# Moving the first normalisation's aggregation to GpSimd, pairing two small operations, and a new instruction order in a one-core attention and feed-forward kernel

## The chip, the cores and the metric

The kernel runs on one core of one Trainium2 chip. The metric is the device time of one execution in microseconds (us): 80.45 us is the median of three runs before the change (80.34 to 80.68). The five engines are called as in the profile: PE (TensorE, matrix products), DVE (VectorE), ACT (ScalarE), POOL (GpSimd) and SP (SyncE, which here only issues DMAs). Each runs its own list of instructions strictly in the order written, and they meet only through semaphores.

## What is computed

x is 4 x 256 x 256, the context 4 x 256 x 128. `fp8` is rounding to float8 e4m3, simulated in float32.

```python
def layernorm(x, eps=1e-5): return (x - mean(x)) / sqrt(var(x) + eps)

def attention(xn, ctx, Wq, bq, Wk, bk):
    q, k = ctx @ Wq.T + bq, ctx @ Wk.T + bk        # 256 x 128 for each of 4 batches
    a = softmax(q @ k.T)
    return xn @ a.T                                 # 256 x 256

def quantised_linear(qx, sx, sc, W, idx):           # rows of W scaled to 448 and rounded to fp8
    ws = max(abs(W[:, idx]), axis=1) / 448
    return qx * sx @ (fp8(W[:, idx] / ws) * ws).T * sc

def ffn(x):                                         # hidden size 704
    qx, sx, sc = quantise(x, up_index)              # per row: peak, scale to 448, round to fp8
    t = silu(quantised_linear(qx, ..., w_gate)) * quantised_linear(qx, ..., w_up)
    return quantised_linear(*quantise(t, down_index), w_down)

x = x + attention(layernorm(x), ctx, ...)
x = x + ffn(layernorm(x))
```

## The kernel before

The 1024 rows of x are 8 tiles of 128 rows (T = 8, two per batch: LT = 2); HB = 2 batches make a half, so most small row statistics are handled for four tiles at once. The hidden size of 704 makes KC = 6 chunks of 128 of the gate and up weights.

There are two stages. **The front** (about the first 37 us) does attention for four batches and, woven between, quantises the weights. For each batch b: `scores(b)` on PE, `score_max(b)` on DVE, `exps(b)` on ACT, `reciprocal_of_z(b)` and `spread_of_z(b)` on DVE (the identity times 1/z, one 128 x 128 block for each half of the rows), `transpose_att(b)` on PE (a product with that block, which transposes and divides at once), `evac_attT(b)` on ACT, `attend(b)` on PE, and `residual(b)` on DVE, which multiplies by the first normalisation's `rstd1` and adds x. `rstd1` needs `bn_stats1` and `bn_aggr1` on DVE and `add_eps1` and `rstd1_of` on POOL. Then the second normalisation (`bn_stats2`, `bn_aggr2`, `centre_x1`), the row peaks and the rounding of x (`grids_x`, `add_grid_x` on DVE, `subtract_x(b)` on POOL), `transpose_qx(b)` on PE and `evac_qxT(b)` on ACT. Each weight chunk k goes `peak_of_up` and `scales_up` (DVE), `scale_up` (ACT), `exponents_up` and `floor_up` (DVE, in pairs of chunks), `add_grid_up` and `subtract_up(k)` (POOL, 128 x 512), `dequantise` (ACT), `transpose_up` (PE), `evac_up` (ACT) and `split_up` (DVE). The down weights are peaked by `peak_of_down`, rounded, transposed by DMA, permuted by POOL's six indirect DMAs (`scatter`) and read back from DRAM (lines 331 to 333).

**The loop over tiles** (from about 37.5 us) starts with `gates(0)`, which waits for `evac_qxT(0)` and for the last `split_up(5)`. For each tile i: `gates(i)` and `ups(i)` on PE (16 products of 352 columns), `silu(i)` on ACT, `hidden(i)`, `peak_of_t`, `reciprocal_t`, `scales_t`, `grids_t`, `add_grid_t` on DVE, `subtract_t(i)` on POOL, `transpose_t(i)` on PE, `evac_tT(i)` on ACT, `down(i)` on PE, `scale_y(i)` on DVE (with `yscale_of(i)` from POOL: row factor times peak), and `add_residual(i)` on POOL or DVE. `keep_clock`, `keep_warm` and `keep_busy` are products on zeros whose results nobody reads.

The order on every engine is written out by hand as a list of calls at the end of each engine's function (POOL from line 438, ACT from 619, DVE from 954, PE from 1283, SP's loads from 308). An instruction waits at the head of its queue until its semaphores are up, and all behind it wait as well.

## Time and profile before

| | |
|---|---|
| median of 3 runs | 80.45 us (80.34 to 80.68) |
| the profiled execution's own time | 80.45 us |
| its span, first to last instruction | 78.6 us |
| outside the span | 1.85 us |
| busy: PE, DVE, ACT, POOL | 69.5, 69.1, 52.0, 54.1 us |
| instructions of DVE and of POOL | 180 and 66 |
| granted clock | 1.00 |

A duration in the profile is from the start of an instruction to the end of its writes, and instructions of one engine overlap a little, so the room that an instruction takes on its engine is read from its start to the next one's start. That distance is called its slot in this document. Matrix products are pipelined, so a busy PE need not be PE at its peak.

### The profile page before, as it was taken

Reading aid. Unit: us, or ns where it says so; the run is one execution under the profiler, and the core shown is the slowest. Engines: PE = TensorE matmul, PEld = TensorE weight load, DVE = VectorE, ACT = ScalarE, POOL = GpSimd, SP = SyncE. Lnnn points to the kernel's source line nnn. Section 1 sums busy time; section 2 is a strip of 40 time slices with the busy share of each in tenths; the row PEclk is TensorE's granted clock in tenths of the full one; section 3 lists DMA queues with packets and bytes.
Section 4 is the critical chain, followed back from the end, with each engine's and each line's share of the span. In section 5 each row is a group of like instructions: output and inputs, shape, how many; then the busy total and the mean of one; then the engine's idle time right before and its main releaser. Section 6 shows DMA issues by size and latency. Waiting matters only on the chain.

```text
span 78.6 us, 1481 instructions
## 1 busy us (share of the span) xinstructions
PE 69.5 (88%) x449; PEld 57.7 (73%) x449; DVE 69.1 (88%) x180; ACT 52.0 (66%) x102; POOL 54.1 (69%) x66
## 2 busy tenths in 40 slices
PE   4999998999749599294999999999799999985996
PEld 4945837988549489272998999979698699744575
DVE  1019999999899999999999999999999999999860
ACT  0615799999966999897877472937924557446400
POOL 5000008973999999985687989899954667985960
DMA  0899999900000000004140201110033001030143
GB/s 18 289 389 388 330 360 397 379 20 0 0 4 4 0 0 8 0 0 91 32 77 0 75 0 33 33 38 0 17 88 112 4 22 53 0 133 0 41 159 133
DMA packets 6839, 7.33 MB, mean 93 GB/s; under 512 B 2256, under 2 KB 5200, under 8 KB 6832
## 3 DMA queue, kind: packets, MB, share of 16 engines
q1 hardware_dynamic: 6064, 5.97, 23.1%
q10 hardware_dynamic: 576, 0.92, 3.3%
q0 software_dynamic: 192, 0.36, 1.5%
q8 instruction: 3, 0.05, 0.3%
q14 instruction: 4, 0.03, 0.1%
HBM read 5.44 MB, written 1.41 MB: 87 GB/s over the span
## 4 chain that ended last, share of the span: by engine, by line
DVE 30%; POOL 25%; PE 22%; issue 15%; DMA 6%; SPq 1%; POOLq 0%; DVEq 0%
POOL q_w L407 6%; DVE t_sb L885 6%; DMA x_sb<-x_dram 6%; PE gate_ps L1197 5%; PE up_ps L1197 5%; DVE peak_w L820 4%; POOL rstd L371 3%; PE gate_ps L1269 3%; POOL sum_w L403 3%; POOL x_sb L435 3%; POOL yscale L417 2%; DVE grid_w L772 2%; PE bank_c L1154 2%; POOL q_t L424 2%; DVE peak_d L850 2%
## 5 line engine op out<-in xcount | busy, mean ns | idle before, releaser
L403 POOL TENSOR_TENSOR sum_w<-sum_w,grid_w 128x512 f32<-128x512 f32 x5 | 5.7, 1155 | 11.9 <-DVE grid_w L777 11.9
L424 POOL TENSOR_TENSOR q_t<-sum_t,grid_t 128x704 bf16<-128x704 f32 x7 | 10.9, 1554 | 3.9 <-DVE sum_t L915 3.9
L1197 PE MATMUL gate_ps<-w_hi,qxT 128*128 128x352 f32 x32 | 10.7, 337 | 1.2 <-issue 1.2
L1197 PE MATMUL up_ps<-w_hi,qxT 128*128 128x352 f32 x32 | 10.8, 340 | 0.4 <-DVE t_sb L885 0.4
L590 ACT ACTIVATE act_g<-gate_ps,rowscale 128x704 f32<-128x704 f32 x8 | 6.7, 843 | 5.3 <-PE gate_ps L1197 5.3
L1197 PE MATMUL gate_ps<-w_lo,qxT 128*128 128x352 f32 x32 | 10.3, 323 | 0.0
L1197 PE MATMUL up_ps<-w_lo,qxT 128*128 128x352 f32 x32 | 10.3, 323 | 0.0
L604 ACT ACTIVATE tT<-bank_b 128x768 bf16<-128x768 bf16 x7 | 5.7, 809 | 5.6 <-PE bank_c L1241 3.2
L1154 PE MATMUL bank_c<-attT,xT 128*128 128x256 f32 x32 | 7.7, 383 | 1.5 <-DVE x L758 1.5
L357 POOL DMA_INDIRECT wdnT_order<-wdnT,idx_sb x6 | 7.0, 1164 | 1.6 <-issue 1.6
L597 ACT ACTIVATE abs_t<-t_sb 128x704 bf16<-128x704 f32 x8 | 6.3, 786 | 2.4 <-DVE t_sb L885 2.4
L1154 PEld LDWEIGHTS bank_c<-attT,xT 128*128 128x128 f32 x32 | 5.8, 190 | 2.4 <-issue 1.7
L1197 PEld LDWEIGHTS gate_ps<-w_hi,qxT 128*128 128x128 f32 x32 | 6.0, 188 | 1.7 <-issue 1.4
L885 DVE TENSOR_TENSOR t_sb<-up_ps,act_g 128x704 f32<-128x704 f32 x8 | 7.1, 887 | 0.1
L915 DVE SCALAR_TENSOR_TENSOR sum_t<-t_sb,s_t,grid_t 128x704 f32<-128x704 f32 x7 | 6.9, 984 | 0.3
L890 DVE TENSOR_REDUCE peak_t<-t_sb 128x1 f32<-128x704 f32 x8 | 7.0, 881 | 0.0
L713 DVE BATCH_NORM_STATS2 bn<-x_sb 128x6 f32<-128x256 f32 x8 | 3.0, 413 | 4.5 <-DMA x_sb<-x_dram 4.5
L407 POOL TENSOR_TENSOR q_w<-sum_w,grid_w 128x512 bf16<-128x512 f32 x6 | 6.8, 1161 | 0.2
L1197 PEld LDWEIGHTS up_ps<-w_hi,qxT 128*128 128x128 f32 x32 | 6.0, 188 | 0.8 <-ACT qxT L547 0.7
L1197 PEld LDWEIGHTS up_ps<-w_lo,qxT 128*128 128x128 f32 x32 | 6.0, 188 | 0.0
L1197 PEld LDWEIGHTS gate_ps<-w_lo,qxT 128*128 128x128 f32 x32 | 6.0, 188 | 0.0
L566 ACT ACTIVATE sum_w<-q_w,peak_w 128x256 f32<-128x256 bf16 x12 | 5.2, 507 | 1.1 <-POOL q_w L407 1.1
(105 smaller groups left out, 190.8 us busy)
## 6 DMA issues: line engine op xcount, KB each, us to landing
x_sb<-x_dram SPq DMA_DIRECT2D x4, 256.0 KB, 8.7
xT<-x_t_dram SPq DMA_DIRECT2D x2, 512.0 KB, 8.9
out_dram<-x_sb SPq DMA_DIRECT2D x8, 128.0 KB, 1.7
wup_sb<-w_gate_up_dram ACTq DMA_DIRECT2D x3, 256.0 KB, 5.7
wup_sb<-w_gate_up_dram SPq DMA_DIRECT2D x3, 256.0 KB, 5.9
wdn_sb<-w_down_dram SPq DMA_DIRECT2D x1, 704.0 KB, 9.3
ctx_sb<-ctx_t_dram SPq DMA_DIRECT2D x2, 256.0 KB, 4.8
wdnT_in_order<-wdnT_order SPq DMA_DIRECT2D x1, 320.0 KB, 2.8
```

Of the source, the lines that this page charges most:

```text
L357: nc.gpsimd.indirect_dma_start(out=wdnT_order, out_offset=bass.IndirectOffsetOnAxis(ap=idx_sb[0:fresh[k], k:k + 1], axis=0), in_=wdnT[0:fr ...
L403: nc.gpsimd.tensor_tensor(sum_w[:, k], sum_w[:, k], grid_w[:, k], ALU.add).then_inc(sum_w_done[k], 1)
L407: nc.gpsimd.tensor_tensor(q_w[:, k], sum_w[:, k], grid_w[:, k], ALU.subtract).then_inc(q_w_done, 1)
L424: nc.gpsimd.tensor_tensor(q_t[:, i % 2], sum_t[:, i % 2], grid_t[:, i % 2], ALU.subtract)\
L590: nc.scalar.activation(halves(act_g[:, i % 3]), gate_ps[:, :, 0:IH], ACT.Silu, scale=rowscale[:, i:i + 1]).then_inc(silu_done, 1)
L597: nc.scalar.activation(abs_t[:, i % 2], t_sb[:, i % 2], ACT.Abs, scale=GRID)\
L604: nc.scalar.activation(tT[:, i % 2], tT_ps, ACT.Copy).then_inc(tT_evac, 1)
L885: nc.vector.tensor_tensor(halves(t_sb[:, i % 2]), up_ps[:, :, 0:IH], halves(act_g[:, i % 3]), ALU.mult).then_inc(t_done, 1)
L890: nc.vector.tensor_reduce(peak_t[:, i:i + 1], t_sb[:, i % 2], AX_X, ALU.max, apply_absolute_value=True).then_inc(peak_t_done, 1)
L915: nc.vector.scalar_tensor_tensor(sum_t[:, j], t_sb[:, j], s_t[:, col], grid_t[:, j], ALU.mult, ALU.add)\
L1154: last = nc.tensor.matmul(xm_ps[:, j], xT[:, b, c, j * P:(j + 1) * P], attT[:, b, c], start=(c == 0), stop=(c == NC - 1))
L1197: last = nc.tensor.matmul(ps[:, h, 0:IH], qxT[:, b, c, j * P:(j + 1) * P].bitcast(F32R), w[:, c, a, h * IH:(h + 1) * IH].bitcast(F32R), st ...
```

## The change

It has four parts. (1) `bn_aggr1` is gone from DVE (8 instructions). POOL makes the variance itself from the raw statistics of four tiles at once, with five small instructions in place of one (`sum_of_halves`, `halves_apart`, `square_apart`, `weigh_apart`, `add_eps1`); it gives N times the variance, and the factor is put back where `attT` is copied out (`evac_attT` now scales by sqrt(N), with the mean's constant to match). (2) `spread_of_z` is one 128 x 256 product with broadcast operands in place of two of 128 x 128. (3) `yscale_of` handles tiles 0 to 5 in pairs, so there are 5 instructions in place of 8. (4) The order of the calls changes on all engines, and three of SP's loads swap places.

```diff
+        apart1 = sb("apart1", [P, T])
+        both1 = sb("both1", [P, T])
+        square1 = sb("square1", [P, T])
...
             load_up(5)
+            load_down()
             load_x(1)
-            load_down()
+            load_x(3)
             load_x(2)
-            load_x(3)
             load_xT(1)
...
-            def add_eps1(h):
+            def halves_apart(h):
                 four = slice(HB * LT * h, HB * LT * (h + 1))
                 pool.wait_ge(stats1_done, HB * (h + 1))
-                step(nc.gpsimd.tensor_scalar(ve1[:, four], mv1[:, four, 1], LN_EPS, 1.0, ALU.add, ALU.mult),
-                     ("ve1", h))
+                step(nc.gpsimd.tensor_tensor(apart1[:, four], bn1[:, four, 1], bn1[:, four, 4], ALU.subtract),
+                     ("apart1", h))
+
+            def sum_of_halves(h):
+                four = slice(HB * LT * h, HB * LT * (h + 1))
+                pool.wait_ge(stats1_done, HB * (h + 1))
+                step(nc.gpsimd.tensor_tensor(both1[:, four], bn1[:, four, 2], bn1[:, four, 5], ALU.add), ("both1", h))
+
+            def square_apart(h):
+                four = slice(HB * LT * h, HB * LT * (h + 1))
+                after(("apart1", h))
+                step(nc.gpsimd.tensor_tensor(square1[:, four], apart1[:, four], apart1[:, four], ALU.mult),
+                     ("square1", h))
+
+            def weigh_apart(h):
+                four = slice(HB * LT * h, HB * LT * (h + 1))
+                after(("square1", h))
+                step(nc.gpsimd.tensor_scalar(square1[:, four], square1[:, four], N / 4.0, N * LN_EPS, ALU.mult, ALU.add),
+                     ("weighed1", h))
+
+            def add_eps1(h):
+                four = slice(HB * LT * h, HB * LT * (h + 1))
+                after(("weighed1", h))
+                after(("both1", h))
+                step(nc.gpsimd.tensor_tensor(ve1[:, four], both1[:, four], square1[:, four], ALU.add), ("ve1", h))
...
-            def yscale_of(i):
+            def yscale_of(first, last):
...
             add_grid_up(0)
             add_grid_up(1)
             subtract_up(0)
             subtract_up(1)
+            sum_of_halves(0)
+            halves_apart(0)
+            square_apart(0)
+            weigh_apart(0)
             add_eps1(0)
-            add_grid_up(5)
             rstd1_of(0)
             add_grid_up(2)
             subtract_up(2)
+            halves_apart(1)
             add_grid_up(3)
+            square_apart(1)
+            weigh_apart(1)
+            add_grid_up(5)
             subtract_up(3)
             subtract_up(4)
             subtract_up(5)
+            sum_of_halves(1)
             add_eps1(1)
             rstd1_of(1)
             add_eps2(0)
             rstd2_of(0)
+            subtract_x(0)
             rowscale_of(0)
-            subtract_x(0)
...
+            subtract_t(1)
             subtract_x(3)
-            subtract_t(1)
-            yscale_of(0)
-            yscale_of(1)
+            yscale_of(0, 1)
+            yscale_of(2, 3)
             scatter(5)
             subtract_t(2)
             subtract_t(3)
+            yscale_of(4, 5)
             subtract_t(4)
             add_residual(0)
-            yscale_of(2)
+            add_residual(1)
+            yscale_of(6, 6)
             subtract_t(5)
-            yscale_of(3)
-            yscale_of(4)
-            yscale_of(5)
-            yscale_of(6)
-            add_residual(1)
             subtract_t(6)
+            yscale_of(7, 7)
             subtract_last(0)
-            yscale_of(7)
...
-                nc.scalar.activation(attT[:, b], attT_ps, ACT.Identity, bias=minus_mean[:, 0:1])\
+                nc.scalar.activation(attT[:, b], attT_ps, ACT.Identity, bias=minus_mean[:, 0:1],
+                                     scale=float(N) ** 0.5)\
...
-                for j in range(2):
-                    last = nc.vector.tensor_scalar(spread_rz[:, b, j], ident_ps, rz[:, b, j:j + 1], None, ALU.mult)
-                last.then_inc(spread_rz_done[b], 1)
+                nc.vector.tensor_tensor(spread_rz[:, b], ident_ps.unsqueeze(1).to_broadcast([P, 2, P]),
+                                        rz[:, b].unsqueeze(2).to_broadcast([P, 2, P]), ALU.mult)\
+                    .then_inc(spread_rz_done[b], 1)
...
             bn_stats1(0)
-            bn_aggr1(0)
             peak_of_up(0)
             peak_of_up(1)
+            peak_of_up(2)
             reciprocal_up(0)
-            peak_of_up(2)
             scales_up(0)
             peak_of_up(3)
+            reciprocal_up(1)
             peak_of_up(4)
+            scales_up(1)
             score_max(0)
-            reciprocal_up(1)
             exponents_up(0)
+            floor_up(0)
+            peak_of_up(5)
+            reciprocal_of_z(0)
+            spread_of_z(0)
             score_max(1)
...
```

The rest of DVE's new order up to the loop over tiles, as it stands after the change, one call after the other: reciprocal_up(2), peak_of_down, reciprocal_of_z(1), scales_up(2), spread_of_z(1), bn_stats1(1), reciprocal_down, bn_stats1(2), exponents_up(1), scales_down, exponents_up(2), floor_up(1), floor_up(2), bn_stats1(3), residual(0), score_max(2), bn_stats2(0), split_up(0), score_max(3), add_grid_up(4), reciprocal_of_z(2), bn_aggr2(0), spread_of_z(2), residual(1), split_up(1), reciprocal_of_z(3), peak_of_x(0), bn_stats2(1), spread_of_z(3), reciprocal_x(0), bn_aggr2(1), split_up(2), grids_down(0), scales_x(0), grids_down(1), grids_x(0), add_grid_down(0), add_grid_x(0), split_up(3), residual(2), add_grid_down(1), bn_stats2(2), split_up(4), peak_of_x(1), bn_aggr2(2), reciprocal_x(1), residual(3), split_up(5). In the loop, scale_y(1) now stands ahead of scales_t(5), and peak_of_x(3) ahead of hidden(0).

On PE, `place_ident` moves from ahead of `project_k(0)` to behind `scores(0)`. `attend(3)` moves ahead of `transpose_qx(0)`, three `keep_clock(2)` stand ahead of `gates(0)` and those between `gates(2)` and `transpose_t(0)` are gone (their number in all is unchanged), `down(2)` and `transpose_t(4)` move ahead of the `keep_busy` calls, and two `keep_busy` move from the end to ahead of `transpose_t(6)`. On ACT, `dequantise(1)`, `dequantise(2)` and `evac_up(0)` move ahead of `exps(2)` and `exps(3)` (`absolute_down(0)` behind them), and `silu(i)` moves ahead of `absolute_t(i - 1)` for tiles 2 and 4.

## Rows read from the trace of the kernel before

**Rows 1.** The page, its part on busy time of each engine.

```profile
PE 69.5 (88%) x449; PEld 57.7 (73%) x449; DVE 69.1 (88%) x180; ACT 52.0 (66%) x102; POOL 54.1 (69%) x66
```

**Rows 2.** Busy time of each engine by stretches of the span.

```profile
core 0: us, PE busy (x) PEld busy (x) DVE busy (x) ACT busy (x) POOL busy (x), PEclk, DMA share, GB/s
...
20.00:33.00 13.00, 9.18 (x61) 8.07 (x60) 12.64 (x42) 11.65 (x30) 12.43 (x14) 1.00 0.01 3
33.00:37.50 4.50, 3.16 (x20) 2.43 (x20) 4.50 (x14) 3.41 (x7) 3.28 (x3) 1.00 0.23 43
37.50:74.00 36.50, 34.84 (x256) 30.32 (x256) 35.66 (x83) 22.39 (x33) 29.25 (x35) 1.00 0.14 38
```

**Rows 3.** The chain of waits: start us, us, what.

```profile
9.77 0.60 DVE neg_max L737
...
37.53 1.52 PE gate_ps L1197 x8
```

**Rows 4.** DVE's instructions in order of time: start us, busy us, what.

```profile
13.80 0.30 DVE L718 BATCH_NORM_AGGREGATE mv<-bn 128x2 f32<-128x6 f32 x2
14.02 0.14 DVE L764 RECIPROCAL rec_w<-peak_w 128x4 f32<-128x4 f32 x1
...
21.66 0.88 DVE L758 SCALAR_TENSOR_TENSOR x<-bank_c,rstd,x_sb 128x256 f32<-128x256 f32 x2 [0.35 <-POOL rstd L371]
...
25.27 0.86 DVE L758 SCALAR_TENSOR_TENSOR x<-bank_c,rstd,x_sb 128x256 f32<-128x256 f32 x2
...
27.30 0.23 DVE L718 BATCH_NORM_AGGREGATE mv<-bn 128x2 f32<-128x6 f32 x2
27.45 0.58 DVE L749 TENSOR_SCALAR spread_rz<-up_ps,rz 128x128 f32<-128x128 f32 x2
27.94 0.68 DVE L785 TENSOR_REDUCE peak_x<-xT 128x2 f32<-128x512 f32 x1
...
30.12 0.94 DVE L868 SCALAR_TENSOR_TENSOR sum_d<-wdn_sb,s_d,grid_d 128x704 f32<-128x704 f32 x1
...
37.02 0.42 DVE L875 TENSOR_TENSOR w_lo<-bank_a,w_hi 128x256 fp32r<-128x256 f32 x1
37.35 0.24 DVE L718 BATCH_NORM_AGGREGATE mv<-bn 128x2 f32<-128x6 f32 x2
...
75.56 0.48 DVE L946 SCALAR_TENSOR_TENSOR y_sb<-bank_a,yscale,down_scale 128x256 f32<-128x256 f32 x1 [0.47 <-PE bank_a L1259]
```

**Rows 5.** POOL's instructions in order of time: start us, busy us, what.

```profile
12.14 2.27 POOL L403 TENSOR_TENSOR sum_w<-sum_w,grid_w 128x512 f32<-128x512 f32 x2 [10.25 <-DVE grid_w L777]
...
16.75 0.58 POOL L365 TENSOR_SCALAR ve<-mv 128x4 f32<-128x4 f32 x1
18.94 1.16 POOL L403 TENSOR_TENSOR sum_w<-sum_w,grid_w 128x512 f32<-128x512 f32 x1 [1.62 <-DVE grid_w L777]
20.05 1.50 POOL L371 TENSOR_TENSOR rstd<-ve,minus_half 128x4 f32<-128x4 f32 x1
...
28.59 0.19 POOL L365 TENSOR_SCALAR ve<-mv 128x4 f32<-128x4 f32 x1
...
30.13 0.99 POOL L378 TENSOR_SCALAR ve<-mv 128x4 f32<-128x4 f32 x1
...
32.31 0.20 POOL L390 TENSOR_TENSOR rowscale<-rstd,peak_x 128x2 f32<-128x2 f32 x1
32.47 1.16 POOL L396 TENSOR_TENSOR q_x<-sum_x,grid_x 128x512 bf16<-128x512 f32 x1
```

**Rows 6.** Groups of instructions by shape: busy us, mean ns of one.

```profile
L417 POOL TENSOR_TENSOR yscale<-rowscale,peak_t 128x1 f32<-128x1 f32 x8 | 2.7, 361 | 0.0
```

**Rows 7.** The loads' and the down weights' issues on SP's queue.

```profile
4.54 0.47 SPq L303 DMA_DIRECT2D wdn_sb<-w_down_dram  x1
...
57.24 0.39 SPq L331 DMA_DIRECT2D wdnT_in_order<-wdnT_order  x1
```

**Rows 8.** PE, the first product of the down weights.

```profile
60.83 0.93 PE L1241 MATMUL bank_c<-wdnT_in_order,tT 128*128 128x256 bf16 x6
```

More of the change, by code:

```diff
@@ L411, in subtract_down @@
                 nc.gpsimd.tensor_tensor(q_d[:, j, 0:I], sum_d[:, j], grid_d[:, j], ALU.subtract).then_inc(q_d_done, 1)
-            def yscale_of(i):
-                pool.wait_ge(peak_t_done, i + 1)
-                pool.wait_ge(rowscale_done, i // LT + 1)
-                nc.gpsimd.tensor_tensor(yscale[:, i:i + 1], rowscale[:, i:i + 1], peak_t[:, i:i + 1], ALU.mult)\
+            def yscale_of(first, last):
+                tiles = slice(first, last + 1)
+                pool.wait_ge(peak_t_done, last + 1)
+                pool.wait_ge(rowscale_done, last // LT + 1)
+                nc.gpsimd.tensor_tensor(yscale[:, tiles], rowscale[:, tiles], peak_t[:, tiles], ALU.mult)\
                     .then_inc(yscale_done, 1)
@@ L661, in _ @@
             evac_qxT(0)
+            evac_up(5)
             absolute_x(1)
-            evac_up(5)
             centre_x1(2)
+            centre_x1(3)
+            silu(0)
             absolute_x(2)
-            silu(0)
-            centre_x1(3)
             silu(1)
@@ L722, in bn_stats1 @@
                 dve.wait_ge(x_in[b], 16)
-                bn_stats(1, x_sb, bn1, b)
-            def bn_aggr1(b):
-                bn_aggr(1, bn1, mv1, stats1_done, b)
+                for j in range(LT):
+                    last = nc.vector.bn_stats(bn1[:, LT * b + j], x_sb[:, b, j])
+                last.then_inc(stats1_done, 1)
             def bn_stats2(b):
@@ L980, in _ @@
             spread_of_z(1)
-            peak_of_down()
+            bn_stats1(1)
             reciprocal_down()
+            bn_stats1(2)
             exponents_up(1)
             scales_down()
+            exponents_up(2)
             floor_up(1)
-            exponents_up(2)
             floor_up(2)
+            bn_stats1(3)
+            residual(0)
             score_max(2)
+            bn_stats2(0)
+            split_up(0)
             score_max(3)
             add_grid_up(4)
-            bn_stats1(2)
-            residual(0)
-            bn_aggr1(2)
-            bn_stats2(0)
-            split_up(0)
             reciprocal_of_z(2)
-            reciprocal_of_z(3)
             bn_aggr2(0)
             spread_of_z(2)
-            bn_stats1(3)
             residual(1)
             split_up(1)
+            reciprocal_of_z(3)
+            peak_of_x(0)
             bn_stats2(1)
-            bn_aggr1(3)
             spread_of_z(3)
-            peak_of_x(0)
+            reciprocal_x(0)
             bn_aggr2(1)
-            reciprocal_x(0)
+            split_up(2)
             grids_down(0)
             scales_x(0)
-            split_up(2)
+            grids_down(1)
             grids_x(0)
             add_grid_down(0)
-            grids_down(1)
             add_grid_x(0)
@@ L1017, in _ @@
             residual(2)
-            peak_of_x(1)
+            add_grid_down(1)
             bn_stats2(2)
             split_up(4)
-            add_grid_down(1)
+            peak_of_x(1)
+            bn_aggr2(2)
             reciprocal_x(1)
@@ L1024, in _ @@
             split_up(5)
-            bn_aggr2(2)
             bn_stats2(3)
@@ L1284, in _ @@
             keep_warm(WARM_UP)
-            place_ident()
             project_k(0)
@@ L1289, in _ @@
             scores(0)
+            place_ident()
             scores(1)
@@ L1293, in _ @@
             keep_clock(2)
-            keep_clock(2)
             transpose_att(0)
@@ L1297, in _ @@
             keep_clock(2)
+            spread()
             transpose_att(1)
-            spread()
+            attend(0)
             scores(2)
+            transpose_up(0)
             scores(3)
-            attend(0)
-            transpose_up(0)
             attend(1)
             transpose_up(1)
+            keep_clock(2)
+            keep_clock(2)
             transpose_att(2)
             transpose_up(2)
-            attend(2)
             keep_clock(2)
             keep_clock(2)
+            attend(2)
             transpose_up(3)
@@ L1313, in _ @@
             transpose_up(4)
+            attend(3)
             transpose_qx(0)
-            attend(3)
             transpose_up(5)
+            keep_clock(2)
+            keep_clock(2)
+            keep_clock(2)
             gates(0)
@@ L1345, in _ @@
             ups(7)
+            down(2)
+            transpose_t(4)
             keep_busy(0)
             keep_busy(1)
-            transpose_t(4)
-            down(2)
             keep_busy(2)
+            transpose_t(5)
             down(3)
             down(4)
-            transpose_t(5)
+            keep_busy(3)
+            keep_busy(4)
             transpose_t(6)
```

83 lines of the change are left out of this document (35 added, 48 removed).

## Prediction

> **What bounds the kernel now.** I began with the page's busy times [rows 1]: PE and DVE stand level at 69 us of a 78.6 us span, POOL at 54. Such shares mix stages, so the busy times by stretch came next [rows 2]. From 20 to 33 us DVE is busy 12.64 of 13.00 us and POOL 12.43; from 33 to 37.5 DVE is busy all 4.50 us, while PE has only 3.16; in the loop over tiles DVE has 35.66 of 36.50 us and PE 34.84. The reader should see that DVE never rests, that POOL runs beside it at the same pressure in the second half of the front, and that PE joins them in the loop. The chain of waits [rows 3] says the same: it runs through DVE's queue at the start (one piece, a score_max of 0.60 us, is shown) and goes through `gates(0)` at 37.53. Last I read DVE's own queue in order of time [rows 4]. `gates(0)` starts right behind DVE's `split_up(5)` (37.02 to 37.44), and the only DVE wait near the end is 0.47 us before the last `scale_y`, at 75.56, behind the tail of transposes and products. So a slot taken out of DVE ahead of 37 us should bring the end forward by as much, unless POOL or PE takes over.
>
> **What the change takes from DVE.** *Aggregation.* Eight instructions go, in four pairs. A pair's slot is 14.02 - 13.80 = 0.22 us or 27.45 - 27.30 = 0.15 us [rows 4]; I count two of each, 0.74 us. *Diagonals.* A pair of 128x128 products has a slot of 27.94 - 27.45 = 0.49 us, four pairs 1.96 us. The 128x256 product that replaces a pair, one operand in PSUM and both broadcast, is not in the trace. The nearest row is L875's 128x256 form, also a tensor_tensor with one operand in PSUM: 37.35 - 37.02 = 0.33 us of slot. The upper bound is L758, a 256-column product from PSUM with a third operand, two in 0.86 us, or 0.43 each. I take 0.33, since the operation and the memory agree: 4 x (0.49 - 0.33) = 0.64 us saved, at the upper bound 0.24. A gain beyond 0.33 has no row for it; the small DVE instructions alone take 0.15 us and 256 columns cannot be cheaper than 128 (half a pair, 0.25), which gives at most 0.96. DVE loses 1.38 us in all (0.98 to 1.70). Dropping the semaphore steps between the `bn_stats1` pairs I cost at nothing, either way: they ran back to back.
>
> **What it adds to POOL.** POOL gets ten small instructions in place of two [rows 5]. Their prices in the trace spread widely: `ve` (128x4) took 0.58, 0.19 and 0.99 us, `rowscale` 0.20, the eight `yscale` 0.36 on average [rows 6]. I take 0.36 and 0.08 for the waits between them, 0.44 each; the bounds are 0.20 and 0.99. The first five fall where POOL idled anyway, 1.62 us ahead of the `add_grid_up` at 18.94 [rows 5], and POOL now starts earlier: of what DVE did ahead of `floor_up(0)`, a pair of `bn_aggr1` (0.22) and `score_max(1)` (0.60) [rows 3] are gone or later and a `scales_up` (0.07) is added, so POOL's first `add_grid_up` comes at about 12.14 - 0.75 = 11.4. Four products of 1.14 bring it to 15.95, which is also about when DVE has done `bn_stats1(1)`. Five small ones take it to 18.1 and the power of 0.9 to 1.5 us [rows 5] to 19.0 to 19.6, where it was 21.55. DVE reaches `residual(0)` at about 19.3; behind it all of DVE's queue would wait, at most 0.3 us, and before it waited 0.35 at the same place [rows 4]. (Where DVE stands in the new order I get by adding up the slots of its new list.)
>
> From 19.3 POOL has, up to the end of `subtract_x(0)`: three `add_grid_up` and four `subtract_up` of about 1.15 (8.05), five small (2.2), the power `rstd1(1)` (1.25), `ve2` (1.0 as at 30.13), `rstd2` (1.1) and `subtract_x(0)` (1.15), together 14.75, so 34.05. Before it was 32.47 + 1.16 = 33.63. `rowscale(0)` (0.20) is moved behind it, which is in the sum. So the small instructions use up the lead that POOL won. What waits for it: `transpose_qx(0)` on PE, now behind `attend(3)`, and behind that `transpose_up(5)`, then ACT's `evac_qxT(0)` and `evac_up(5)`, then `split_up(5)`: by the rows of their kind 0.4 + 0.6 + 0.5 + 0.4 + 0.4, so 2.3 us to 36.35. DVE's own queue would be through `split_up(5)` at 37.44 - 1.38 = 36.06, and it carries one `bn_aggr2` (0.15) earlier than before: 36.2. POOL is thus late by about 0.15 to 0.4 us, and that is what I take back from the saving.
>
> **Edits at nothing.** *Loads.* `load_down` is issued ahead of `load_x(1)`, and `load_x(3)` ahead of `load_x(2)`. They are issued from 4.54 us on [rows 7]. The w_down data comes earlier by one x load, and so does its reader: `peak_of_down` now stands ahead of `bn_stats1(1)`. The x load that is now last is read by `bn_stats1(2)`, near 16 us. If DVE met data still in flight, it would lose some tenths; I count none. *`yscale` in pairs.* Three fewer small POOL instructions, and none of them between `subtract_t(5)` and `subtract_t(6)`. This opens room on POOL in a stage where DVE sets the pace, so no gain. *Down weights.* They are read back from 57.24 [rows 7] and first used at 60.83 [rows 8]. The `scatter` chain hangs on POOL; it keeps its length and starts with `subtract_down(1)`, which no longer waits as long for DVE. To come 1.0 us forward in the loop, `down(0)` needs this chain about 0.5 us earlier, an estimate; POOL gets there by about 0.8. *`keep_clock` and `place_ident`.* The same number of filler products, three sets now ahead of `gates(0)`; PE has 1.3 us free there [rows 2]. *`scale_y(1)`* moves forward ahead of `scales_t(5)`; it takes a slot of 0.4 that DVE pays either way, and `down(1)` is just done then.
>
> **The sum.** 1.38 saved on DVE, less 0.35 for `split_up(5)` held by POOL's late `subtract_x(0)` and small new waits in the loop: 1.03 us. The profiled execution took 80.45 us, 1.85 of it outside its span, and the median is the same 80.45. Forecast **79.4 us**, a span of 77.6.
>
> **Rivals.**
> *A, forecast (0.52):* DVE's saved slots come through but for some tenths; 78.9 to 79.9.
> *B, the gain is not passed on (0.20):* another queue holds the loop where it was. For it: PE is at 34.84 of 36.50 us there, close behind DVE [rows 2], and the down weights come only just ahead of `down(0)`. If the read-back does not move, the loop can gain no more than about 0.5 us; with the upper bound for the diagonals (0.4 less) nothing measurable is left. 80.0 to 80.7, middle 80.3. Against it: PE's filler products leave it slack.
> *C, slower by POOL's small instructions (0.14):* five of them stand between `rstd1(0)` and `rstd1(1)`, where POOL is full. At 0.99 each (30.13, while DVE ran the two-input product of 30.12 to 31.06 [rows 4, 5]) instead of 0.44 they add 2.75 us, `split_up(5)` ends at 39.1 in place of 37.44, and the time is 80.45 + 1.7 = 82.1. The point at which it decides: `subtract_x(0)` must end later than 35.1, that is the five must cost 0.66 each with their waits; the mean of the twelve priced above is 0.40, so 0.48 with a wait. The first five would do the same to `residual(0)`. The Trainium skill's "GPSIMD Engine Reference" (section 8, Key points) says that GpSimd shares its SBUF interfaces with VectorE and is held up by VectorE instructions in a 2-port mode or with two SBUF inputs. By that rule the new DVE order, dense in such instructions, speaks against the change; the 0.99 beside 0.19 agrees with it, but the 1.15 us products alongside keep their length, so the hold seems to last one DVE instruction, at a start.
> *D, PE's clock (0.04):* the fillers between `gates(2)` and `transpose_t(0)` are gone. If PE fell to its lower level (1.2 of 2.4 GHz) there, each group of eight products would take 1.5 us more [rows 3]; with two or three of them, 82 to 84. Against it: with PE busy 3.16 of 4.50 us the granted clock stayed at 1.00 [rows 2].
> *E, the order brings more (0.10):* the peak of the last x tile and the sums stand earlier, the tail has no POOL clog; another 0.6 to 1.2 us, about 78.5.
>
> **The numbers.** 0.5% is 0.4 us, about what a measurement of this kernel tells from no change; so faster is below 80.05, slower above 80.85. Faster: A 0.52, E 0.10, a quarter of B 0.05, making 0.67. Same: the rest of B, 0.15. Slower: C and D with 0.18. The likeliest case's own range is 78.9 to 79.9. The range that holds 8 in 10 takes in B and half of E and the mild part of C: 78.4 to 80.9.
>
> **What the profile after would show.** `bn_aggr` x8 in place of x16; the diagonals x4 at 0.42 us each; POOL's first `add_grid_up` at 11.4; `rstd1(0)` ending at 19.0 to 19.6 and no DVE wait over 0.4 at the first `residual`; `subtract_x(0)` ending near 34; `gates(0)` at 36.5; the first `hidden` near 39.5; DVE's busy time at 67.7. The prediction is wrong if the small POOL instructions average over 0.6 us, if the broadcast product takes over 0.6, if DVE shows new waits of together 1 us, or if the loop from `gates(0)` to the end grows.

## The result: 81.05 us after, 80.50 us before

The changed kernel took 81.05 us (median of 20 runs, 80.34 to 82.60), the kernel before 80.50 us on the same chips (20 runs, 80.26 to 81.04). The ratio is 1.0059, with a 95% interval of 1.0033 to 1.0085: slower by 0.6%. The forecast was 79.4 us with a range of 78.4 to 80.9. Some executions of each of these kernels take one to two microseconds longer than the rest, and every ratio in this document leaves out those that are more than 1.5% above their kernel's fastest, while the medians count all.

The profiled execution took 81.35 us, with a span of 79.5. Its page, the part on busy time:

```profile
PE 68.5 (86%) x449; PEld 56.7 (71%) x449; DVE 69.1 (87%) x168; ACT 52.3 (66%) x102; POOL 57.2 (72%) x71
```

DVE executes twelve instructions fewer than in [rows 1] and is busy for the same 69.1 us; POOL has 57.2 in place of 54.1. By stretches, as in [rows 2]:

```profile
core 0: us, PE busy (x) PEld busy (x) DVE busy (x) ACT busy (x) POOL busy (x), PEclk, DMA share, GB/s
...
20.00:33.00 13.00, 10.41 (x67) 8.54 (x66) 12.61 (x35) 11.67 (x29) 12.37 (x17) 1.00 0.01 3
33.00:37.50 4.50, 3.92 (x28) 3.27 (x27) 4.50 (x12) 3.63 (x7) 4.50 (x4) 1.00 0.00 0
37.50:74.00 36.50, 33.54 (x246) 28.98 (x245) 35.59 (x82) 22.22 (x33) 29.03 (x31) 1.00 0.15 44
```

From 33 to 37.5 us POOL is now busy all 4.50 us, as DVE is; in the loop DVE is as full as before (35.59 us, it was 35.66) and PE has more room (33.54, it was 34.84), in part because its four filler calls there moved ahead of the loop. The two groups of new DVE instructions, with busy time and mean ns of one:

```profile
L783 DVE TENSOR_TENSOR spread_rz<-up_ps,rz 128x256 f32<-128x256 f32 x4 | 1.6, 407 | 0.0
...
L753 DVE BATCH_NORM_AGGREGATE mv<-bn 128x2 f32<-128x6 f32 x8 | 0.9, 154 | 0.0
```

So four products for the diagonals at 0.41 us each, and eight aggregations in place of sixteen. The saving is there; most of what took it back are instructions that got longer. DVE in order of time (what answers to [rows 4]):

```profile
20.39 0.88 DVE L793 SCALAR_TENSOR_TENSOR x<-bank_c,rstd,x_sb 128x256 f32<-128x256 f32 x2 [0.64 <-POOL rstd L399]
...
28.72 0.88 DVE L816 TENSOR_SCALAR grid_d<-abs_d,s_d 128x704 bf16<-128x704 bf16 x1
...
29.59 0.39 DVE L816 TENSOR_SCALAR grid_d<-abs_d,s_d 128x704 bf16<-128x704 bf16 x1
...
33.34 1.44 DVE L903 SCALAR_TENSOR_TENSOR sum_d<-wdn_sb,s_d,grid_d 128x704 f32<-128x704 f32 x1
...
37.52 0.41 DVE L910 TENSOR_TENSOR w_lo<-bank_a,w_hi 128x256 fp32r<-128x256 f32 x1
...
45.37 0.81 DVE L816 TENSOR_SCALAR grid_t<-abs_t,s_t 128x704 bf16<-128x704 bf16 x1
...
48.82 1.13 DVE L816 TENSOR_SCALAR grid_x<-abs_x,s_x 128x256 bf16<-128x256 bf16 x2
```

POOL over the same time (what answers to [rows 5]):

```profile
12.01 2.27 POOL L431 TENSOR_TENSOR sum_w<-sum_w,grid_w 128x512 f32<-128x512 f32 x2 [10.12 <-DVE grid_w L812]
...
17.23 0.58 POOL L386 TENSOR_SCALAR square<-square 128x4 f32<-128x4 f32 x1
17.89 1.25 POOL L394 TENSOR_TENSOR ve<-both,square 128x4 f32<-128x4 f32 x1
19.22 1.05 POOL L399 TENSOR_TENSOR rstd<-ve,minus_half 128x4 f32<-128x4 f32 x1
...
26.00 3.40 POOL L435 TENSOR_TENSOR q_w<-sum_w,grid_w 128x512 bf16<-128x512 f32 x3
...
32.87 1.16 POOL L424 TENSOR_TENSOR q_x<-sum_x,grid_x 128x512 bf16<-128x512 f32 x1
...
44.80 1.18 POOL L424 TENSOR_TENSOR q_x<-sum_x,grid_x 128x512 bf16<-128x512 f32 x1
...
48.13 1.53 POOL L453 TENSOR_TENSOR q_t<-sum_t,grid_t 128x704 bf16<-128x704 f32 x1
```

Read the two side by side. `grids_down(0)` at 28.72 took 0.88 us, its twin at 29.59 took 0.39. POOL's three products run to 29.40, and 28.72 + 0.88 is 29.60. `add_grid_down(1)` at 33.34 took 1.44 us where [rows 4] have 0.94 for this shape; POOL's `q_x` runs from 32.87 to 34.03, and DVE ends at 34.78. The first gives the rule and the second follows it: DVE ends one instruction's own length after a point 0.19 us ahead of POOL's recorded end, 29.40 - 0.19 + 0.39 = 29.60 and 34.03 - 0.19 + 0.94 = 34.78. `grid_t` at 45.37 (0.81) and `grid_x` at 48.82 (1.13 for two) lie beside POOL's products of 44.80 and 48.13 in the same way, and the same sum gives their ends.

The ledger at `split_up(5)`, which starts at 37.52 and not at 37.02 [rows 4], comes from differences of DVE's slots (start to next start). Saved: the aggregations 0.74 and the diagonals 0.70. Lost: `grids_down(0)` 0.49, `add_grid_down(1)` 0.50, `add_grid_up(4)` 0.10, the wait before `residual(0)` 0.29, waits for loads at the start 0.25, `bn_aggr2(2)` moved ahead 0.16, and 0.15 in small pieces. The sum is +0.50. From `split_up(5)` to the end of the span it takes 79.5 - 37.52 = 41.98 us, where it was 78.6 - 37.02 = 41.58: another 0.40. Together 0.9, which is the difference of the spans. The two medians differ by 0.55 us only, since the profiled execution of the changed kernel took 0.3 us more than its median.

### The profile page after: what moved, and what is told of

Its sections match the earlier page's. It is cut to its first block, busy times and chain, and to the rows that moved or that the text cites. A ratio compares the mean times of both kernels' runs of the same rounds, so it can differ in the third digit from the quotient of the medians.

```text
span 79.5 us, 1473 instructions
## 1 busy us (share of the span) xinstructions
PE 68.5 (86%) x449; PEld 56.7 (71%) x449; DVE 69.1 (87%) x168; ACT 52.3 (66%) x102; POOL 57.2 (72%) x71
## 4 chain that ended last, share of the span: by engine, by line
DVE 45%; PE 25%; POOL 10%; issue 8%; DMA 7%; SPq 1%; ACT 1%; DVEq 0%; POOLq 0%
DMA wup_sb<-w_gate_up_dram 7%; PE up_ps L1228 5%; PE gate_ps L1300 5%; DVE t_sb L920 4%; DVE x L793 4%; PE bank_c L1272 4%; DVE w_lo L910 4%; PE gate_ps L1228 4%; DVE bn L748 3%; PE bank_a L1272 3%; DVE grid_x L816 3%; DVE peak_w L855 3%; DVE peak_x L820 3%; DVE sum_x L848 3%; POOL sum_w L431 3%
## 5 line engine op out<-in xcount | busy, mean ns | idle before, releaser
L359 POOL DMA_INDIRECT wdnT_order<-wdnT,idx_sb x6 | 7.8, 1293 | 1.3 <-issue 1.3
L1307 PE MATMUL bank_b<-warm_w 128*128 128x128 f32 x40 | 5.4, 278 | 1.7 <-ACT kT L549 1.7
L1307 PEld LDWEIGHTS bank_b<-warm_w 128*128 128x128 f32 x40 | 4.9, 192 | 2.5 <-ACT kT L549 2.5
L593 ACT ACTIVATE sum_w<-wup_sb,s_w 128x256 f32<-128x256 f32 x12 | 5.1, 498 | 1.5 <-DVE s_w L803 1.5
```

What stands on the lines that cost most here:

```text
L359: nc.gpsimd.indirect_dma_start(out=wdnT_order, out_offset=bass.IndirectOffsetOnAxis(ap=idx_sb[0:fresh[k], k:k + 1], axis=0), in_=wdnT[0:fr ...
L1307: nc.tensor.matmul(bank_b[:, 0, 0:P], warm_w[:, :], warm_w[:, :], start=True, stop=True)
```

## The experiments

Two theories stood against each other at first. *Exclusion*: while a POOL product runs, a DVE instruction of certain forms can't proceed, and so what DVE saves turns into stretched instructions whenever the phase between the two queues is bad. *Order*: the new order costs by itself, whatever the three parts bring. A third came up on the way: PE's clock.

**The disputed mechanism alone.** Behind the end of the kernel, DVE runs four rounds of six instructions; eight POOL subtractions start behind the second. (The output tiles are complete by then; the added results are not used.)

```diff
+ pool.wait_ge(probe_go, 1)
+ for v, k in spare:
+     nc.gpsimd.tensor_tensor(v[:, k * I:(k + 1) * I], wdn_sb[:, 0], wdn_sb[:, 1], ALU.subtract)
...
+ tensor_reduce(peaks[..], left)              # 128x512 f32, one SBUF operand
+ tensor_tensor(sum_w[:, n], left, right)     # 128x512 f32, two SBUF operands
+ tensor_scalar(rounded[..], abs_d[:, 0])     # 128x704 bf16
+ tensor_tensor(sum_w[..], y_ps[1], right[:, 0])  # 128x256, one PSUM operand
```

> The kernel before, with a row of extra instructions behind its end whose results nobody reads; the time is not the point, their durations are. DVE runs four rounds of: reduction, product of two SBUF operands (512 columns, float32), reduction, scaling of bf16 (704 columns), reduction, product of a PSUM and an SBUF operand (256 columns). Beside the last two rounds POOL runs eight subtractions of 704 columns. Theory of exclusion (DVE instructions with two SBUF operands, or scaling bf16 in SBUF, wait until POOL's running instruction is over, and the other way round): reductions and the PSUM product keep their length in all four rounds (about 0.68 and 0.42 us), while the two-operand product (0.6 to 0.7 alone) and the scaling (0.4 alone) grow by up to 1.3 us each beside POOL, and end at POOL's instruction ends. Rival, the one of the prediction (only a start is held, by one short DVE instruction): all DVE lengths stay within 0.1 us of their first rounds.

DVE in order of time, first alone, then beside POOL:

```profile
82.13 0.68 DVE L1116 TENSOR_TENSOR sum_w<-wup_sb 128x512 f32<-128x512 f32 x1
...
83.32 0.33 DVE L1118 TENSOR_SCALAR q_w<-abs_d 128x704 bf16<-128x704 bf16 x1
83.57 0.68 DVE L1119 TENSOR_REDUCE mv<-wup_sb 128x1 f32<-128x512 f32 x1
84.17 0.41 DVE L1120 TENSOR_TENSOR sum_w<-bank_a,wup_sb 128x256 f32<-128x256 f32 x1
...
85.09 1.78 DVE L1116 TENSOR_TENSOR sum_w<-wup_sb 128x512 f32<-128x512 f32 x1
86.80 0.67 DVE L1117 TENSOR_REDUCE mv<-wup_sb 128x1 f32<-128x512 f32 x1
87.39 1.21 DVE L1118 TENSOR_SCALAR q_w<-abs_d 128x704 bf16<-128x704 bf16 x1
...
89.11 0.41 DVE L1120 TENSOR_TENSOR sum_w<-bank_a,wup_sb 128x256 f32<-128x256 f32 x1
...
90.04 0.67 DVE L1116 TENSOR_TENSOR sum_w<-wup_sb 128x512 f32<-128x512 f32 x1
```

In the third round the product of two SBUF operands goes from 0.68 to 1.78 us and the bf16 scaling from 0.33 to 1.21; the reduction (0.68, 0.67) and the product with a PSUM operand (0.41, 0.41) don't change. In the fourth round the scaling takes 1.21 again, but the product of two SBUF operands, at 90.04, keeps its 0.67: it started just ahead of a product of POOL's, and that one got longer in its place. It is the second line here; the others give shortest, median and longest of a group of POOL's products in ns:

```profile
L509 POOL TENSOR_TENSOR grid_w<-wdn_sb x4: 1667/1939/2147, 84.7 to 90.1; 128x704 bf16<-128x704 f32 x4
...
90.10 2.15 POOL L509 TENSOR_TENSOR grid_w<-wdn_sb 128x704 bf16<-128x704 f32 x1
...
L509 POOL TENSOR_TENSOR q_x<-wdn_sb x2: 1662/1662/1662, 95.6 to 97.2; 128x704 bf16<-128x704 f32 x2
```

POOL's product takes 1.66 us undisturbed, up to 2.15 when it has to wait for DVE. Exclusion holds, in both directions, by the form of the DVE instruction and by which of the two starts first. The rule with the 0.19 us gives the ends of 86.87 and 88.60 to within 0.06 us. The rival, all lengths within 0.1 us, is out.

**The order alone**: before's operations in the new order.

```diff
# the call lists of the changed kernel with the old bodies; on DVE:
+ peak_of_x(3)
  hidden(0)
...
# and on PE:
- transpose_qx(0)
  attend(3)
+ transpose_qx(0)
  transpose_up(5)
+ keep_clock(2)
```

> The operations of before in the order of after (bn_aggr1 right behind each bn_stats1, two diagonals each, one yscale after the other). If the new order is what costs (collisions of DVE with POOL's products, waits for loads and for rstd1), this is slower than before by the parts' saving on top of what after lost: 81.5 to 82.3 us. Rival, POOL's five small instructions are the loss: this is 80.0 to 80.8, faster than after.

82.37 us (median of 6 runs): one run of 81.02 and five from 82.35 to 82.48, no ratio, beside 80.97 for the kernel before (19 runs up to 81.52 and four from 81.80 to 82.32). The median is where the order theory put it, and the one shorter run is no slower than the kernel before. In the profile, a run of 82.44, DVE waited 0.85 us for the first scores near 11 us. The changed kernel, profiled again, had the same wait (0.92) and stood 1.0 us later at `split_up(5)` than in its first profile (38.51, 37.52), with the same stretches; so this much belongs to the execution. Without it, `split_up(5)` at 38.59 becomes about 37.7, against 37.02, but what the order costs ahead of the loop isn't shown by one such trace. The loop behind it took 80.6 - 38.59 = 42.01 us, 0.43 more than before, and the two traces of the changed kernel have the same: 41.98 and 41.99.

**One part alone, in the old order.** The diagonals, and then the aggregation:

```diff
- spread_of_z: two tensor_scalar 128x128 per tile      (diagonals)
+ spread_of_z: one tensor_tensor 128x256, broadcast
...
- bn_aggr1(0..3) on DVE                                (aggregation)
+ sum_of_halves, halves_apart, square_apart, weigh_apart on POOL
```

> Before with the one change that spread_of_z is one product. DVE's queue loses 0.7 us in the front. If DVE's slots are passed on to the end, 79.8; if other waits take them back (collisions with POOL move about), 80.2 to 80.6.

80.34 us against 80.97, ratio 0.9924 (0.9893 to 0.9955).

> Before with bn_aggr1 given to POOL, old order, the five small instructions in a row where add_eps1 was. DVE loses 0.74 us. Theory that POOL's small instructions are dear: rstd1(0) and the chain to subtract_x(0) come 1 to 2 us later, 81 to 82. Theory of exclusion on the long ones only: five small ones add 1.5 us to a full POOL, of which subtract_x(0) has little to spare: 80.5 to 81.3. If POOL has the room after all: 79.8.

80.14 us, ratio 0.9905 (0.9874 to 0.9937). Each part alone is faster than the kernel before, by 0.8% and 1.0%, which is 0.6 to 0.8 us. The aggregation alone is the best version found. The row factors in pairs and the swapped loads were not measured by themselves.

**All three parts in the old order.**

> Before with the aggregation on POOL, the diagonals and the row factors in pairs, and the old order on all engines. Theory that the new order alone is what costs: the two gains measured apart (0.95% and 0.76%) add up, about 79.2 to 79.6 when before is 80.5. Rival, both gains fill the same gap (another engine's chain holds the loop): no better than 0.95% faster than before.

82.40 us (median of 13 runs): four runs between 80.44 and 80.83, nine from 82.07 to 83.31; ratio 0.9964 (0.9909 to 1.0019). The gains don't add, not even by the ratio, where the sum of the two would be 0.983. The profile, a run of 83.31, shows two meetings of DVE and POOL that each part alone avoids. The first, with the aggregation alone and then with all parts:

```profile
30.83 1.04 POOL L399 TENSOR_TENSOR rstd<-ve,minus_half 128x4 f32<-128x4 f32 x1
...
31.10 0.94 DVE L905 SCALAR_TENSOR_TENSOR sum_d<-wdn_sb,s_d,grid_d 128x704 f32<-128x704 f32 x1
...
30.81 0.94 DVE L903 SCALAR_TENSOR_TENSOR sum_d<-wdn_sb,s_d,grid_d 128x704 f32<-128x704 f32 x1
...
30.86 1.78 POOL L399 TENSOR_TENSOR rstd<-ve,minus_half 128x4 f32<-128x4 f32 x1
```

With the diagonals shorter as well, `sum_d` starts 0.05 us ahead of POOL's power and not behind it, and the power takes 1.78 us in place of 1.04. So POOL is late for what follows:

```profile
35.35 1.52 POOL L439 TENSOR_TENSOR q_d<-sum_d,grid_d 128x704 bf16<-128x704 f32 x1
```

DVE beside it:

```profile
36.00 1.61 DVE L903 SCALAR_TENSOR_TENSOR sum_d<-wdn_sb,s_d,grid_d 128x704 f32<-128x704 f32 x1
...
39.35 0.88 DVE L793 SCALAR_TENSOR_TENSOR x<-bank_c,rstd,x_sb 128x256 f32<-128x256 f32 x2 [1.66 <-PE bank_c L1185]
```

The second `sum_d` meets `q_d` (36.87 - 0.19 + 0.93 is 37.61, as measured). In the kernel before it had just ended:

```profile
33.58 1.53 POOL L411 TENSOR_TENSOR q_d<-sum_d,grid_d 128x704 bf16<-128x704 f32 x1
...
35.31 0.94 DVE L868 SCALAR_TENSOR_TENSOR sum_d<-wdn_sb,s_d,grid_d 128x704 f32<-128x704 f32 x1
```

Here POOL is 1.8 us later than that and DVE only 0.7, and the miss has become a hit. With the aggregation alone it was still a miss: `q_d` ended at 36.11, `sum_d` started at 36.30 and took 0.93. Then DVE waits 1.66 us for PE:

```profile
35.45 0.40 PE L1197 MATMUL bank_d<-identb,q_x 128*128 128x128 bf16 x4 [1.22 <-POOL q_x L424]
35.69 3.63 PE L1185 MATMUL bank_c<-attT,xT 128*128 128x256 f32 x8
```

PE idled 1.22 us twice, before the product at 33.61 and here, and then did the eight products of `attend(3)` in 3.63 us, where the changed kernel's took 1.97; the granted clock was 0.81 from 33 to 42 us and 0.50 to 0.55 from 35.7 to 39.3. This is the prediction's rival D in another place: behind two idle stretches PE ran at the lower of its two levels, 1.2 GHz. Six of the 13 runs had a mean clock of 0.979 and not 1.000, and took 82.51 to 83.31; the other three of the nine took 82.07 to 82.40 at full clock, so the clock is not all of it. None of the four runs below 80.9 was profiled.

**The changed kernel again, and with the aggregation back on DVE** (order, diagonals and row factors as changed).

```diff
+ bn_aggr1(b) behind each bn_stats1(b), on DVE
- sum_of_halves, halves_apart, square_apart, weigh_apart (0 and 1), on POOL
```

> The changed kernel again, beside the others of this set on the same chip. All theories: 0.3 to 0.9% slower than before.

81.48 us, ratio 1.0041 (1.0004 to 1.0078).

> After with the aggregation back on DVE (new order, pairs kept). Theory of the new order: 0.7 us of DVE slots come back and nothing is won, so slower than after by 0.4 to 0.9 us. Rival, the small POOL instructions are what makes after slow in the new order (rstd1(0) late): equal to after or faster.

80.36 us, ratio 0.9958 (0.9919 to 0.9997). In this order, taking the aggregation away from POOL makes the kernel 0.8% faster by the two ratios, some 0.7 us (1.1 by the medians), though DVE has 0.74 us more to do. DVE:

```profile
28.73 0.39 DVE L779 TENSOR_SCALAR grid_d<-abs_d,s_d 128x704 bf16<-128x704 bf16 x1
...
32.85 0.93 DVE L866 SCALAR_TENSOR_TENSOR sum_d<-wdn_sb,s_d,grid_d 128x704 f32<-128x704 f32 x1
...
47.84 1.13 DVE L779 TENSOR_SCALAR grid_x<-abs_x,s_x 128x256 bf16<-128x256 bf16 x2
```

No wait at `residual(0)`, 0.39 and 0.93 us for the two instructions that were stretched, `split_up(5)` at 36.54. But `grid_x` is still held at 47.84, as in the run with the order alone, and the loop still takes 42.06.

**Swaps.** Three DVE calls change places, so that three instructions of the forms that POOL holds up miss its products.

```diff
- split_up(2); grids_down(0); scales_x(0)
+ grids_down(0); split_up(2); scales_x(0)
...
- residual(2); add_grid_down(1)
+ add_grid_down(1); residual(2)
...
- grids_x(3) ... peak_of_t(2)
+ peak_of_t(2); grids_x(3)
```

> After with three places of DVE's order changed: grids_down(0) ahead of split_up(2), add_grid_down(1) ahead of residual(2), peak_of_t(2) ahead of grids_x(3). By the theory of exclusion these three DVE instructions no longer wait for the end of a POOL product (0.48, 0.50 and 0.65 us in the profile of after): up to 1.6 us faster than after, at least 0.6, POOL's products being held a little in turn. Rival, those waits only took the place of later ones on PE or POOL: within 0.3 us of after.

82.28 us (80.75 to 83.71), ratio 1.0009 (0.9956 to 1.0061), not distinguishable from the changed kernel's 1.0041. The three stretches are gone, and most of the gain has not come: POOL's `q_x` now waits in its turn, 1.64 us for 1.16. The same stretch as in the window above, with the same columns, shows where more of it went in the profiled run, of 82.30:

```profile
33.00:37.50 4.50, 3.88 (x16) 3.27 (x17) 3.49 (x11) 2.31 (x4) 3.96 (x5) 0.67 0.19 44
```

The clock is 0.67 there, and DVE is busy 3.49 of 4.50 us; it waits 0.84 for PE's `attend(3)` and 0.82 for ACT behind it. Only 2 of the 12 runs had a mean clock below 1, though. To see how much of it was the clock, six filler products were put ahead of `attend(3)`, here and in the kernel with all parts in the old order (where `attend(3)` also moves ahead of `transpose_qx(0)`):

```diff
  transpose_up(4)
+ keep_clock(6)
  attend(3)
  transpose_qx(0)
```

> The kernel with the three swaps on DVE (median 82.28, profiled run 82.30), with six filler products (keep_clock(6)) added in PE's queue ahead of attend(3). In the run without them PE idled 1.35 and 1.02 us ahead of attend(3), the granted clock from 33 to 37.5 us was 0.67, the eight products took 2.83 us where the changed kernel has 1.97, and DVE waited 0.84 for them at residual(3) and 0.82 at split_up(5). Clock theory: the granted clock is 1.00, attend(3) takes 1.6 to 2.0 us, both waits go down to 0.3 or less together, and the median falls by 1.0 to 1.7 us, to 80.6 to 81.3; the repairs of the swaps then show. Rival (the clock fell in 2 of 12 runs only, and the rest of the time went to small waits between DVE and POOL that the swaps moved): the median stays within 0.5 us of 82.28.

> All three parts in the old order, with two edits in PE's queue: six filler products (keep_clock(6)) ahead of attend(3), and attend(3) ahead of transpose_qx(0). Without them the profiled run took 83.31 us: PE idled 1.22 us twice between 32.4 and 35.5, the eight products of attend(3) took 3.63 us, twice their usual length per product, and residual(3) and split_up(5) came late. Clock theory: the granted clock is 1.00 throughout in every run, attend(3) takes 1.6 to 2.0 us and ends before 36, DVE waits under 0.3 us at residual(3), split_up(5) is at 37 to 37.5 in place of 40.21, and the median falls from 82.4 to 80.0 to 80.7. Rival (the wait for POOL's late subtract_x(0) and the stretched DVE products hold the front by themselves, and the clock only fell because PE had nothing to do): the clock is 1.00 but split_up(5) stays later than 38.5 and the median above 81.3.

82.07 us (4 runs) and 82.01 us (4 runs), ratios 1.0150 (1.0097 to 1.0202) and 1.0134 (1.0081 to 1.0186). The clock stayed at 1.00 in all eight runs and the eight products took 1.89 us, which fits that the idle time lets it fall; with four runs each, beside 2 of 12 and 6 of 13 without fillers, it is no proof. `split_up(5)` came earlier, at 37.70 for 38.18 and at 38.20 for 40.21. But the medians fell by 0.2 and 0.4 us only, where the clock theory had expected 1.0 to 2.4, and the ratios rose, from 1.0009 and 0.9964: by these ratios the kernels with fillers are slower, by more than 1 us, than the shorter runs of those without, in which the clock mostly held anyway. They hold PE's queue for 1.50 us, so `attend(3)` starts at 34.64 where the swaps alone have 33.62, and the best run of the second kernel took 81.54 where the one without fillers had four below 80.9. In it both meetings are as before, 1.79 us for POOL's power and 1.63 for `sum_d`. The clock is a real cost in the runs that have it, and not the whole. Fewer fillers were not tried.

**One repair in the loop**: the kernel with the aggregation on DVE, with the third swap only.

> The kernel with the aggregation back on DVE, with one more edit: peak_of_t(2), a reduction with one SBUF operand, is called ahead of grids_x(3) in DVE's queue and not behind add_grid_t(1). In that earlier kernel's profile DVE's bf16 scaling in grids_x(3) at 48.00 held a slot of 1.05 us where the kernel before has 0.40, beside POOL's product q_t. Theory 1 (a DVE bf16 scaling is held until a running POOL product ends, a reduction is not): the slot is back at 0.40, peak_of_t(2) keeps its 0.80, and the time falls by about 0.6 us, from a median of 80.36 to about 79.7, a ratio to before of 0.982 to 0.990. Rival (the loop is bound by something else, PE's products or the read-back of the down weights, and the stretched instruction only fills a wait): the slot is repaired and the time stays within 0.2 us of 80.36.

81.11 us (10 runs), ratio 1.0027 (0.9991 to 1.0063). The repaired pair took 0.47 us, as foreseen; the loop got no shorter, 42.25 us, because others are stretched in its place:

```profile
49.95 0.63 DVE L779 TENSOR_SCALAR grid_t<-abs_t,s_t 128x704 bf16<-128x704 bf16 x1
...
54.33 0.82 DVE L779 TENSOR_SCALAR grid_t<-abs_t,s_t 128x704 bf16<-128x704 bf16 x1
```

Both `grid_t` have 0.40 undisturbed. Neither the theory's 79.7 nor the rival's 80.36 came true. In the profiled run `split_up(5)` stood at 37.15 and not at 36.54, with no stretch more in front of it.

**The old loop behind the new front**: all queues in the old order from `gates(0)` on; once with the changed front, once with the aggregation on DVE.

```diff
  gates(0)
- ...the new order of PE, DVE, POOL and ACT from here on
+ ...the old order of PE, DVE, POOL and ACT from here on
```

> The changed kernel with the old order of all queues from gates(0) on (on DVE from behind split_up(5), on PE from behind gates(0), with the old places of the filler products there, on POOL from behind subtract_down(0), on ACT from behind evac_up(5)), and the row factors one tile at a time as before. The front is that of the changed kernel. In the runs with the new order the loop has the same stretched instructions whatever the parts: scales_t(0) and grids_t(0) 0.19 and 0.20 us longer, grids_x(3) 0.65 longer, add_grid_t(4) and scale_y(6) 0.22 and 0.24, in the run with only the order changed as well. From split_up(5) to the end of the span it takes 42.0 to 42.1 us, against 41.6 in the kernel before. Order theory: those slots are back at their old lengths and the loop takes 41.6; the time falls by 0.4 to 0.6 us from 81.05 to 81.48, to 80.5 to 81.0. Rival (the stretch comes from the phase in which DVE leaves the front, not from the order of the loop): other instructions are stretched, grids_t, add_grid_t or scale_y, by together 0.5 us or more, and the time stays within 0.2 us.

> The new order up to gates(0) with the diagonals in pairs, the aggregation on DVE, and the old order from gates(0) on with single row factors. The kernel with the new loop took 80.36 us (median), with split_up(5) at 36.54, 0.48 ahead of the kernel before, and then a loop of 42.1 us, 0.5 longer than before. Order theory: the loop is back at 41.6 and the time falls to 79.7 to 80.0, a ratio to before of 0.985 to 0.992, faster than both kernels. Rival (phase): the loop stays at 42 us with other instructions stretched and the time at 80.2 or more.

83.57 us (4 runs, 81.59 to 84.59, no ratio) and 83.21 us (4 runs), ratio 1.0296 (1.0237 to 1.0354). Neither theory's time came true. Both kernels carry the fillers of the new front and of the old loop, eight products more than before. All four runs of the first and two of the second had a mean clock of 0.979; in the first's profile the granted clock was 0.50 from 76 to 78 us, behind 1.33 us in which PE idled. The second's profile, at a clock of 1.00, is read here. Up to 62 us the order theory's part is right: `grids_t(0)` and `grids_x(3)` have their old slots in both, and the second kernel does its first `scale_y` at 62.32, before at 62.60. Then comes this, on PE:

```profile
61.22 0.92 PE L1241 MATMUL bank_c<-wdnT_in_order,tT 128*128 128x256 bf16 x6 [0.51 <-issue]
```

on DVE:

```profile
66.22 0.89 DVE L885 TENSOR_TENSOR t_sb<-up_ps,act_g 128x704 f32<-128x704 f32 x1 [0.37 <-PE up_ps L1197]
...
67.53 1.38 DVE L915 SCALAR_TENSOR_TENSOR sum_t<-t_sb,s_t,grid_t 128x704 f32<-128x704 f32 x1
...
69.34 1.45 DVE L951 TENSOR_TENSOR x_sb<-y_sb,x 128x256 f32<-128x256 f32 x1
```

and on POOL:

```profile
67.44 0.72 POOL L435 TENSOR_TENSOR x_sb<-y_sb,x 128x256 f32<-128x256 f32 x1
...
68.99 1.52 POOL L424 TENSOR_TENSOR q_t<-sum_t,grid_t 128x704 bf16<-128x704 f32 x1 [0.83 <-DVE sum_t L915]
```

The last part of the down weights' read-back took 3.7 us where the kernel before has 2.6, and `down(0)` starts 0.51 us late. Why the transfer took longer stays open. `hidden(7)` waits 0.37 us for PE behind it and starts at 66.22, 0.32 later than before. Then `sum_t` takes 1.38 us and not 0.98, beside POOL's addition, and `x_sb` 1.45 and not 0.58, beside `q_t`. A lag of 0.32 us has become 1.60 by DVE's last instruction, and two stretches are all of the difference (0.40 + 0.87). Another 1.2 us lies behind it, up to the end of the span (3.7 us, it was 2.5), in the last store; open like the read-back.

## Why the prediction was wrong, step by step

*What DVE saves.* Right. Predicted 0.74 and 0.64 us, measured 0.74 and 0.70.

*The first POOL chain.* Wrong by 0.7 to 1.3 us. It began at 12.01 and not 11.4; 0.25 us of that are DVE's longer waits for loads at the start, which the prediction counted as none (whether the swapped loads made them isn't shown). The two last of its five small instructions took 0.58 and 1.25 us, beside DVE's uint16 and bf16 forms of L807 and L812, which run back to back up to 19.09. `rstd1(0)` ended at 20.27, predicted 19.0 to 19.6, and `residual(0)` waited 0.64. (The lower price of the power, 0.9, stands in no row: the shortest in the trace of before is 1.01, and it took 1.05.) The small instructions as a whole were priced rightly (0.41 us on average over ten, assumed 0.36): which of them sits beside a dense stretch of DVE decides, not the mean.

*`subtract_x(0)` at 34.05.* Right, 34.03. It is not what held `split_up(5)`: DVE came to that instruction late and started it without a wait. So the 0.15 to 0.4 us that the prediction took back for it were the wrong term.

*DVE's own queue.* This is the step that failed. The sum took every DVE slot as constant: "DVE's own queue would be through `split_up(5)` at 37.44 - 1.38 = 36.06". In place of it 0.99 us of stretch came in at two instructions, and 0.10 at a third, and `split_up(5)` started 0.50 us later than before, not 1.0 to 1.4 earlier. The text of rival C had the rule and read it one way only: "the 1.15 us products alongside keep their length, so the hold seems to last one DVE instruction, at a start". It asked what DVE does to POOL and not what POOL does to DVE; the key point that it cites speaks of contention and doesn't say who is held up. The Trainium skill has the other half in "SBUF — State Buffer" (SBUF: two separate sides): the port pair that the two share is an exclusive lock, whichever starts first has it for its whole instruction, and the other blocks. The prediction drew on another of its pages and not on this one. The probe agrees with it for POOL's large products: 0.68 became 1.78 us on DVE, and 1.66 became 2.15 on POOL. For POOL's small powers the traces show no hold over the whole recorded time, and there they decide: with the aggregation alone, `sum_d` started at 31.10, in the middle of a power of 30.83 to 31.87, and took its own 0.94 us. The other way round the power was held.

The evidence was in the trace of before, and not read. `grid_t` took 0.62 us, and not 0.40, beside `q_x`:

```profile
44.36 1.17 POOL L396 TENSOR_TENSOR q_x<-sum_x,grid_x 128x512 bf16<-128x512 f32 x1
...
45.12 0.62 DVE L781 TENSOR_SCALAR grid_t<-abs_t,s_t 128x704 bf16<-128x704 bf16 x1
```

In the same way `sum_t` at 57.15 took 1.15 beside `q_t`, and not 0.95.

*The loop.* It was forecast to keep its length and grew by 0.40 us. The run with the order alone has the same growth (0.43), so the three parts are not needed for it; the stretches at `grid_t` and `grid_x` are the same in both. The order is not the only way to it: in the old order, with all parts and the fillers, the loop took 42.10. What it would be without the stretches isn't settled, since both repairs moved the waits elsewhere.

*Rival B*, the read-back, did not decide in the changed kernel (`down(0)` started without a wait), but its late end began the delay in the last two experiments.

*Rival C* named the sign and the engine. Its price, the small instructions at 0.66 us or more each and `subtract_x(0)` after 35.1, did not occur; the cost came by another route. That the aggregation on POOL is what makes the changed kernel slower in this order is shown: 81.48 with it, 80.36 without, and ratios of 1.0041 and 0.9958 whose intervals don't meet. That it gains in the old order is shown too, 80.14. So it is not a good or bad edit by itself.

*Rivals D and E.* All 20 runs of the changed kernel had a granted clock of 1.00; the clock fell only in runs of other versions, and in their profiles ahead of the loop or near its end. Of E's further gain nothing came: the loop got longer.

What stays open: how much the loads' landing moves these phases from run to run, what the new order costs ahead of the loop, and how much of the missing gain of all three parts in the old order is due to the two meetings that its profile shows.

## What to carry to other kernels

Where two engines exclude each other by the form of their instructions, price an edit by laying the two queues side by side after the edit, not by adding up saved slots; look in the trace for one instruction with two lengths. A tuned order of two such queues is a set of near misses, and a saving of 0.7 us on one of them can cost more than it brings. Measure the parts of a change one by one: here two of them gained 0.8% and 1.0% alone, and with the third added, in the same order, 0.4% within an interval that takes in nothing, while the median of all runs was 1.4 us longer.

## What the runs showed of the hardware that was not expected

A DVE instruction with two SBUF operands, or a bf16 scaling, that starts while a POOL product runs proceeds about 0.19 us ahead of POOL's recorded end and then takes its own length: 1.78 for 0.68, 1.21 for 0.33, 1.44 for 0.94 us. If it starts 0.06 us ahead of POOL it keeps its length and POOL is held (0.67, beside 2.15 for 1.66). It counts as busy all the while, so DVE's busy time, 69.1 us before and after, hid the loss. Reductions and forms with a PSUM operand are free of it (0.67 and 0.41 us, unchanged), and so is the new 128x256 product of the diagonals, at 0.39 to 0.42. A small power on POOL did not hold `sum_d` (0.94 us at 31.10), but was held by it (1.78 for 1.04).
